# Recurrence stage: GpSimd builds an item's tree right after its decays, the limits follow the next item's statistics, and two norms of norms come from one variance

## The reference

```python
x = x + _L0_attn_ref(_layernorm(x), ...)   # its own layer norm again, projections, softplus, a state scan of 64 states a channel
x = x + _L0_ffn_ref(_layernorm(x), ...)    # x @ expert_w[0].T + expert_b[0]
x = x + _L1_attn_ref(_layernorm(x), ...)   # layer norm again, k, v, sigmoid decays and reads; per head (8 of 64 x 64):
                                           #   state = (1 - w_t)[:, None] * state + k_t v_t ;  out = r_t . state
x = x + _L1_ffn_ref(_layernorm(x), ...)    # layer norm again, signs -> best of 8 clusters, best of its 8 tiles (argmax),
                                           #   the row's 8 values of that tile, min and max of each tile over all rows, a spline
```

## Time and profile before

| what | value |
|---|---|
| median of 3 runs | 8956.1 us (8954.75 to 8961.61) |
| the profiled execution's own time | 8956.13 us |
| its span in the profile | 8954.3 us |
| busy over the span | PE 7718.1 us (86%), DVE 7107.0 (79%), POOL 5805.7 (65%), ACT 4707.2 (53%) |
| pre stage, 0 to 560 us | DVE 305.55 us busy, PE 338.37, POOL 32.64 |
| scan stage, 600 to 5560 us | DVE 4801.94 us busy, POOL 4779.56, PE 4554.60 |
| mid stage, 5571 to 7073 us | PE 1432.18 us busy, DVE 438.29, granted clock 0.99 |
| recurrence stage, 7092 to 8732 us | DVE 1395.19 us busy, PE 1290.36, POOL 779.33, granted clock 0.79 |

### The profile page before, as it was taken

The page is one execution under the profiler, slowest core; times in us unless marked ns, Lnnn a source line. Parts: engine busy times, 40 slices in busy tenths (PEclk is TensorE's granted clock), DMA queues, the critical chain, the costliest instruction groups (busy, mean ns, idle before and its releaser), DMA issues. The chain is left out here.

```text
span 8954.3 us, 223728 instructions
## 1 busy us (share of the span) xinstructions
PE 7718.1 (86%) x76550; PEld 5688.4 (64%) x76550; DVE 7107.0 (79%) x8782; ACT 4707.2 (53%) x10584; POOL 5805.7 (65%) x3304
## 2 busy tenths in 40 slices
PE   5659989999989899999999998899999877778774
PEld 3337777777777777777777776444444455555552
DVE  5549999999999999999999998323323488888876
ACT  4447777777777777777777776111111122222220
POOL 0019999999999999999999998000000144444444
PEclk8779999999999999999999999999999887777875
DMA  3340000000000000000000001122212211121115
GB/s 129 136 149 0 20 20 19 0 20 20 0 20 20 20 0 20 20 10 9 20 20 0 20 5 58 61 84 75 89 67 88 83 61 60 63 63 63 61 47 172
DMA packets 198781, 423.45 MB, mean 47 GB/s; under 512 B 22448, under 2 KB 48496, under 8 KB 183024
## 3 DMA queue, kind: packets, MB, share of 16 engines
q1 hardware_dynamic: 172768, 382.77, 12.7%
q10 hardware_dynamic: 25872, 38.80, 1.2%
HBM read 225.11 MB, written 196.41 MB: 47 GB/s over the span
## 5 line engine op out<-in xcount | busy, mean ns | idle before, releaser
L453 POOL TENSOR_TENSOR scan_hc<-scan_h,scan_cb 128x1024 f32<-128x1024 f32 x2048 | 4779.6, 2369 | 253.1 <-DMA scan_cb<-scratch_bc 117.6
L619 DVE TENSOR_TENSOR_SCAN scan_h<-scan_a,scan_carry,scan_u 128x512 f32<-128x512 f32 x4096 | 4801.9, 1261 | 156.1 <-PE scan_u L558 125.3
L558 PE MATMUL scan_u<-scan_dg,scan_v 64*128 64x128 f32 x32768 | 2391.7, 286 | 340.0 <-DVE scan_h L619 280.1
L504 ACT ACTIVATE scan_a<-scan_dt,scan_aneg 128x512 f32<-128x512 f32 x4096 | 2659.5, 708 | 44.4 <-issue 30.1
L558 PEld LDWEIGHTS scan_u<-scan_dg,scan_v 64*128 64x128 f32 x32768 | 2000.7, 188 | 820.0 <-DVE scan_h L619 538.1
L566 PE MATMUL scan_y<-scan_ident,scan_hc 128*128 128x128 f32 x16408 | 2250.4, 280 | 59.5 <-POOL scan_hc L453 33.6
L566 PEld LDWEIGHTS scan_y<-scan_ident,scan_hc 128*128 128x128 f32 x16408 | 1764.3, 141 | 309.7 <-POOL scan_hc L453 34.5
L475 ACT ACTIVATE scan_dg<-scan_half,scan_bt 128x64 f32<-128x64 f32 x4096 | 1138.7, 341 | 5.3 <-DVE scan_onward L602 5.2
L144 POOL TENSOR_TENSOR mid_r<-mid_ve,mid_half_neg 128x4 f32<-128x4 f32 x48 | 48.5, 1011 | 1269.0 <-DVE mid_ve L129 1269.0
L496 ACT ACTIVATE scan_carry<-scan_h,scan_onward 128x4 f32 (+1 forms) x1008 | 302.9, 301 | 1043.1 <-DVE scan_h L619 1043.1
L1223 DVE TENSOR_TENSOR core_rk<-core_rr,core_k 128x128 f32<-128x128 f32 (+7 forms) x512 | 409.0, 799 | 0.0
(11 more groups left out here) (211 smaller groups left out, 8209.8 us busy)
## 6 DMA issues: line engine op xcount, KB each, us to landing
scratch_y<-scan_yo ACTq DMA_DIRECT2D x17, 1024.0 KB, 4.7
pre_x<-in_x SPq DMA_DIRECT2D x16, 1024.0 KB, 6.9
scratch_z<-pre_zt SPq DMA_DIRECT2D x16, 1024.0 KB, 3.9
scratch_dt<-pre_dt SPq DMA_DIRECT2D x16, 1024.0 KB, 4.6
scratch_vr<-pre_vr ACTq DMA_DIRECT2D x16, 1024.0 KB, 4.7
scan_dt<-scratch_dt SPq DMA_DIRECT2D x16, 1024.0 KB, 5.3
scan_v<-scratch_vr SPq DMA_DIRECT2D x32, 512.0 KB, 7.7
scan_z<-scratch_z SPq DMA_DIRECT2D x16, 1024.0 KB, 10.7
```

The source lines that it names most:

```text
L453: pool.tensor_tensor(hc[:, q].rearrange("p n (r j) -> p n r j", j=P), h[:, q].rearrange("p n (r j) -> p n r j", j=P), cb[:, bass.ds(b * NS ...
L504: ins = act.activation(a[:, q, n, :], dt[:, par, q, :], ACT.Exp, scale=aneg[:, q, bass.ds(m * 2 + n, 1)])
L558: mm = pe.matmul(u_ps[:, q % 2, g, k * HP:(k + 1) * HP, :], v[row, par, k, q, :], dg[row, buf, k], start=True, stop=True)
L619: ins = dve.tensor_tensor_scan(h[:, q, n, :], a[:, q, n, :], u_ps[:, q % 2, :, :, n].rearrange("p g t -> p (g t)"), carry[:, q, bass.ds(m ...
```

## The change

In `pre_phase` and `mid_phase` the second norm takes no statistics of its own. The mean of a normalized row is 0 and its variance v / (v + eps), so both scalings in one are (x - mean) / sqrt(v (1 + eps) + eps^2). `pre_phase` makes both `ve` rows from one variance (`both_stats`), one root of twice the width, and then `zh` and `z` from x (`both_norms`); the piece with the statistics stands where the first norm stood, and the one with root and rows where the second stood. `mid_phase` calls `norm_dve` once, with `twice`, in place of its third and fourth norm.

In `core_phase` GpSimd makes the tree of item i + 3 in turn i, which is the item whose decays VectorE makes in that same turn. The work is cut in two pieces around `pick`, and `total` is a third piece, one turn later, behind `root`. On VectorE the sum of `pr` and the limits leave `route` and come behind the next item's statistics, before its root is waited for. `pr` is stored element by element instead of tile by tile. All leads of the stage grow by one (the limits have lead 0, the rest 1 to 5); between the other pieces nothing moves. In leads of before, the order in turn i is now: GpSimd `root(i)`, `totals(i+2)`, `keys(i+3)` (five products), `pick(i)`, `more_keys(i+3)` (ten products); VectorE `state(i)`, `norms(i)` (statistics only), `limits(i-1)`, `centred(i)` (L1200 to L1207), `decays(i+3)`, `spread_scores(i+2)`, `route(i)`.

```diff
+NORM_BOTH = 10
+BOTH_VE = 4
+
+
+def both_stats(dve, ticks, cnt, x, st, mv, ve, tiles):
+
+    for j in range(tiles):
+        last = dve.bn_stats(st[:, j, :], x[:, j, :])
+    cnt.link(dve, last)
+    hold(dve, ticks)
+    for j in range(tiles):
+        last = dve.bn_aggr(mv[:, j, :], st[:, j, :])
+    cnt.link(dve, last)
+    cnt.inc(dve.tensor_scalar(ve[:, 0], mv[:, :, 1], EPS, None, ALU.add))
+    cnt.inc(dve.tensor_scalar(ve[:, 1], mv[:, :, 1], 1.0 + EPS, EPS * EPS, ALU.mult, ALU.add))
+
+
+def both_norms(dve, cnt, roots, item, root_n, outs, x, mv, ve, r0, rr, tmp, tiles):
+
+    roots.wait(dve, item, root_n)
+    cnt.link(dve, dve.tensor_tensor(tmp, r0, r0, ALU.mult))
+    cnt.link(dve, dve.tensor_tensor(tmp, tmp, ve, ALU.mult))
+    cnt.link(dve, dve.tensor_scalar(tmp, tmp, -0.5, 1.5, ALU.mult, ALU.add))
+    cnt.link(dve, dve.tensor_tensor(rr, r0, tmp, ALU.mult))
+    for e in (1, 0):
+        for j in range(tiles):
+            last = dve.tensor_scalar(outs[e][:, j, :], x[:, j, :], mv[:, j, 0:1], rr[:, e, j:j + 1], ALU.subtract, ALU.mult)
+        cnt.inc(last)
...
-            def first_norm(c, par, half):
+            def stats(c, par, half):
                 norm_steps.begin(c)
                 dve.wait_ge(x_in[par], (half + 1) * 16)
+                both_stats(dve, ticks_dve, norm_steps, x[:, par], st, mv, ve, J)
+
+            def norms(c, par, half):
 
                 pe_steps.wait_freed(dve, c)
-                norm_dve(dve, ticks_dve, norm_steps, root_steps, c, 1, z[:, par], x[:, par], st, mv, ve[:], r0[:], rr[:], tmp[:], J)
-
-            def second_norm(c, par, half):
-                norm_dve(dve, ticks_dve, norm_steps, root_steps, c, 2, zh[:, par], z[:, par], st, mv, ve[:], r0[:], rr[:], tmp[:], J)
+                both_norms(dve, norm_steps, root_steps, c, 1, (z[:, par], zh[:, par]), x[:, par], mv, ve[:], r0[:], rr[:], tmp[:], J)
...
-            skewed(dve, NCH, [(0, turned), (1, first_norm), (0, copies), (1, second_norm), (0, softplus)])
+            skewed(dve, NCH, [(0, turned), (1, stats), (0, copies), (1, norms), (0, softplus)])
...
-                norm(c, 3, h, x2[:, par])
-                norm(c, 4, x[:, par], h)
+                norm(c, 3, x[:, par], x2[:, par], twice=True)
...
-            pipelined(sp, ITEMS, [(4, load_decays), (2, load_rows), (0, store)])
-            after.wait_all(sp, ITEMS - 1)
+            pipelined(sp, ITEMS, [(5, load_decays), (3, load_rows), (1, store)])
+            routed.wait_all(sp, ITEMS - 1)
...
             def keys(i, par, m):
                 pool_a.begin(i)
 
-                pe_b.wait_freed(pool, i)
-
-                after.wait(pool, i - 2, S_STATE)
+                pe_b.wait(pool, i - 2, B_OUT)
                 chain.wait_all(pool, i)
-
...
-                join(0)
-                half(1, 1)
-                half(1, 0)
+                pool_a.inc(join(0, par))
+                pool_a.inc(half(1, 1, par))
+                pool_a.inc(half(1, 0, par))
                 pool_a.wait(pool, i, 1)
-                join(1)
-                last = widen(1)
+                pool_a.inc(join(1, par))
+                pool_a.inc(widen(1, par))
+
+            def more_keys(i, par, m):
+                last = 5
                 for l in range(2, LEVELS):
                     pool_a.wait(pool, i, last)
-                    join(l)
-                    last = widen(l)
-                    half(l, 1)
-                    half(l, 0)
+                    if l + 1 < LEVELS:
+                        pool_a.inc(join(l, par))
+                    last = pool_a.inc(widen(l, par))
+                    pool_a.inc(half(l, 1, par))
+                    pool_a.inc(half(l, 0, par))
                 pool_a.wait(pool, i, last)
                 for kind, src, dst in ((1, rk[:, par, SUB], steps(kl[:, par])), (0, first[:, par, 0:SUB], ql[:, par])):
                     f = far[LEVELS][:, kind * C:(kind + 1) * C].rearrange("p (o c) -> p o c", o=1).broadcast_to([P, SUB, C])
                     pool_a.inc(pool.tensor_tensor(dst, src, f, ALU.mult))
 
+            def totals(i, par, m):
+                totaled.begin(i)
+
+                after.wait(pool, i - 2, S_STATE)
+                totaled.inc(join(LEVELS - 1, par))
+
             def pick(i, par, m):
 
                 after.wait(pool, i, S_OH)
                 hold(pool, ticks_pool)
-                pool_b.inc(pool.tensor_tensor(pr[:].rearrange("p (n e) -> p n e", e=8), xf[:].rearrange("p (n e) -> p n e", e=8),
+                pool_b.inc(pool.tensor_tensor(pr[:].rearrange("p (e n) -> p n e", e=8), xf[:].rearrange("p (n e) -> p n e", e=8),
                                               oh[:, bass.ds(par * (L // P) + m, 1), :].rearrange("p o (n e) -> p (o n) e", e=1).broadcast_to([P, NT, 8]), ALU.mult))
-            pipelined(pool, ITEMS, [(0, root), (2, keys), (0, pick)])
+            pipelined(pool, ITEMS, [(1, root), (3, totals), (4, keys), (1, pick), (4, more_keys)])
...
-                pool_a.wait_all(dve, i)
+                totaled.wait_all(dve, i)
...
+            def centred(i, par, m):
                 pool_b.wait(dve, i, 1)
...
+            def limits(i, par, m):
+                routed.begin(i)
+                at = lambda t: t[:, bass.ds(par * (L // P) + m, 1), :].rearrange("p o n -> p (o n)")
+
                 pool_b.wait_all(dve, i)
                 hold(dve, ticks_dve)
-                after.link(dve, dve.tensor_reduce(at(xs), pr[:].rearrange("p (n e) -> p e n", e=8), AX.X, ALU.add))
+                routed.link(dve, dve.tensor_reduce(at(xs), pr[:].rearrange("p (e n) -> p e n", e=8), AX.X, ALU.add))
                 hold(dve, ticks_dve)
-                after.inc(dve.tensor_reduce(mm2[:, 0:1], at(xs), AX.X, ALU.max))
-                after.link(dve, dve.tensor_reduce(mm2[:, 1:2], at(xs), AX.X, ALU.min, negate=True))
+                routed.inc(dve.tensor_reduce(mm2[:, 0:1], at(xs), AX.X, ALU.max))
+                routed.link(dve, dve.tensor_reduce(mm2[:, 1:2], at(xs), AX.X, ALU.min, negate=True))
 
                 for e in range(2):
-                    after.inc(dve.scalar_tensor_tensor(out=ext[:, e, :], in0=pen[:], scalar=mm2[:, e:e + 1], in1=ext[:, e, :], op0=ALU.min, op1=ALU.max))
-                after.wait(dve, i, after.n)
-            pipelined(dve, ITEMS, [(0, state), (0, norms), (3, decays), (2, spread_scores), (0, route)])
+                    routed.inc(dve.scalar_tensor_tensor(out=ext[:, e, :], in0=pen[:], scalar=mm2[:, e:e + 1], in1=ext[:, e, :], op0=ALU.min, op1=ALU.max))
+                routed.wait(dve, i, routed.n)
+            pipelined(dve, ITEMS, [(1, state), (1, norms), (0, limits), (1, centred), (4, decays), (3, spread_scores), (1, route)])
...
```

More of the change, by code:

```diff
@@ L117, in hold, with norm_dve @@
     eng.sem_inc(ticks, 1)
-def norm_dve(dve, ticks, cnt, roots, item, root_n, out, x, st, mv, ve, r0, rr, tmp, tiles):
+def norm_dve(dve, ticks, cnt, roots, item, root_n, out, x, st, mv, ve, r0, rr, tmp, tiles, twice=False):
     for j in range(tiles):
@@ L128, in norm_dve @@
     cnt.link(dve, last)
-    cnt.inc(dve.tensor_scalar(ve, mv[:, :, 1], EPS, None, ALU.add))
+    if twice:
+        cnt.inc(dve.tensor_scalar(ve, mv[:, :, 1], 1.0 + EPS, EPS * EPS, ALU.mult, ALU.add))
+    else:
+        cnt.inc(dve.tensor_scalar(ve, mv[:, :, 1], EPS, None, ALU.add))
     roots.wait(dve, item, root_n)
@@ L1097, in root, with join @@
                 pool_b.inc(pool.tensor_tensor(r0[:], ve[:], half_neg[:], ALU.pow))
+            def join(l, par):
+                e = ends(l, par)
+                n = C >> l
+                left, right = e[:, 1:n:2], e[:, n:2 * n:2]
+                if l + 1 == LEVELS:
+                    return pool.tensor_tensor(total[:, par], left, right, ALU.mult)
+                left, right = (t.rearrange("p (c e) -> p c e", e=2) for t in (left, right))
+                return pool.tensor_tensor(pair_ends(joint[l + 1][:]), left, right, ALU.mult)
@@ L1437, in outputs @@
                 pe_b.inc(mm)
-            pipelined(pe, ITEMS, [(1, tree), (1, turn_keys), (2, products), (0, turn_x), (1, reads), (2, turn_scores), (0, tile_scores), (1, sums), (1, outputs)])
+            pipelined(pe, ITEMS, [(2, tree), (2, turn_keys), (3, products), (1, turn_x), (2, reads), (3, turn_scores), (1, tile_scores), (2, sums), (2, outputs)])
 def final_phase(nc, D, N, x3_s, oh_s, xs_s, ext_s, table_d, grid_d, ident_d, out_d):
```

62 lines of the change are left out of this document (28 added, 34 removed).

## The result

The changed kernel takes 8649.8 us (median of 4 runs, 8644.1 to 8653.7), beside it the kernel before 8958.9 (8954.8 to 8963.2): ratio 0.9654, 95% interval 0.9638 to 0.9671. The profiled execution has a span of 8647.0 us.

What follows compares the result with a forecast made beforehand. VectorE's list, stretched beside GpSimd's tree, was taken to set the 25.35 us recurrence turn. From 8956.1 us, 233 (59 turns at 21.4) and 12 (pre and mid) were subtracted: 8711 us, own range 8680 to 8760, wider range 8655 to 8830.

Steps and rivals of the forecast that it cites:

- 12 forecast: Pre and mid: the first item saves 5.1 us and 7.1 us of norm work, together 12 us; steady turns gain nothing.
- Of the rivals the first: Recurrence stage: TensorE becomes the bound at the low clock, its stretch stays at 17.1 us; 8850 us, chance 8%.
- the second (all of VectorE excludes GpSimd): Recurrence stage: every VectorE instruction excludes GpSimd's products, turn 26.8 us, slower at 9032 us; chance 3%.
- the third: Recurrence stage: exclusion moves only in part, tree some 2 us longer in its new place; 8823 us, chance 12%.
- the fifth: Recurrence stage: the tree's new place gives nothing, VectorE's wait equals the old stretching; 8944 us, chance 2%.
- At 13.0, y ends at 6.0: Recurrence turn: TensorE's stretch from `turn_x`, begun at -7.0, takes 13.0 us, so y ends 6.0 us after `own`.
- 11.4 for VectorE to resume: Recurrence turn: after `ve`, limits and GpSimd's root, VectorE starts the Newton pieces 11.4 us behind `own`.
- 21.4: Recurrence stage: mean turn after the change, 21.15 us plus 0.25 for slow TensorE stretches, against 25.35 before.
- the remainder of the turn before: Recurrence turn: adding up the old turn gave 25.1 against 25.35 measured; that 0.25 us was added to the new turn.
- the 60th turn that was not counted: Recurrence stage: of 60 intervals from item 3 to item 63 the first was taken as lost, so 59 counted.
- the forecast's tie: TensorE: slow stretches follow about 6 us of idle ahead of `turn_x`; mean idle falls from 5.2 to 2 us.
- The fourth rival: Recurrence stage: limits hide entirely, no slow stretch, GpSimd alone sets a turn of 20.35 us; 8649 us, chance 10%.

Runs made afterwards that it cites:

- e1: Kernel before with only the norms of norms made from one variance, recurrence stage code unchanged: 8946.0 us, ratio 0.9985 to the kernel before.
- b1: Changed kernel with `ve` made by two instructions with one SBUF tensor each instead of one with two: 8627.9 us.
- e4: Changed kernel with GpSimd's tree back at its old place behind `root`, limits still moved: 8807.8 us.
- e9b: Changed kernel with two added matmuls of 512 columns at the head of `turn_x`, lengthening TensorE's stretch to y: 8688.4 us.
- e8: Kernel before with four added matmuls of 512 columns ahead of TensorE's wait for `xf`, filling its idle time: 8963.4 us in one run.
- b2: Changed kernel with the last two products of GpSimd's tree (`kl` and `ql`) put behind the next turn's root: 8657.8 us.

## Why the prediction was wrong in size

The main mechanism was right: GpSimd's tree no longer lies on VectorE's decays. Row by row: the decays take 7.2 us from first product to `own`, the first of them 0.28, Newton to decays 2.2, tree with `pick` ends 9.7 behind `own`; the wait at the sum of `pr` is gone; root is waited for 1.84 us; `ve` is held (1.41). x3, the statistics and the spread are not stretched. Pre and mid gave 14.2 by e1, 12 forecast. Of the rivals the first is out (stretches over 15 us are 10 of 63, not all), the second (all of VectorE excludes GpSimd) by b1, the third by the tree's end at 9.7, the fifth by e4.

The step that failed is "At 13.0, y ends at 6.0" and what hung on it: TensorE's stretch was taken too long, so the limits were put on the path in every turn, 11.4 for VectorE to resume. Measured, the stretch takes 12.25 us or less in 42 of 63 turns, 20 of these 10.5, which no turn of before had in its steady part. With y at 3.5 to 5.2, in 38 of 60 turns, the limits end 8.5 to 10.0 behind `own`, the root ends last at 10.35, and the turn is 19.8. e9b makes y late again and gets turns of 20.2 to 22.0, mean 21.17. By parts, of the 0.86 us between 21.4 and 20.54: the turn with y at 6.3 is 20.7 where the forecast added up 20.9 and 0.25 for 6.0, so the addition was 0.45 too long or more (0.25 of it is the remainder of the turn before, carried over without a row); the ordinary turns (19.8 and 20.7) have a mean of 20.0, another 0.7 less; and those over 22 us cost 0.55 instead of 0.25. The 0.7 needed the shorter stretch, but not that alone. By the forecast's own terms a turn set by the root would last 10.2 + 0.8 + 2.2 + 7.2 + 0.25 = 20.65; it lasts 19.8, since the root ends at 10.35 and not at 11.0 and nothing of the 0.25 shows. That VectorE resumes at 11.3 in the turn of 20.7, close to the 11.4, is partly luck: `ve` ends at 9.7, not 8.9, held until GpSimd's last product ends, and the limits then need 1.5 us and don't wait for the root. 60 x 0.86 and the 60th turn that was not counted (3.95) are the 56 us missed in the stage.

Why the stretch is shorter shows in the granted clock. Three stretches of the changed kernel, 10.5, 13.3 and 16.7 us long (windows, columns as above):

```profile
7622.60:7633.10 10.50, 10.50 (x85) 7.59 (x87) 9.87 (x27) 2.14 (x4) 3.51 (x7) 1.00 0.26 76
7642.30:7655.60 13.30, 13.27 (x82) 9.24 (x84) 10.09 (x27) 2.14 (x4) 6.22 (x12) 0.74 0.25 79
7682.80:7699.50 16.70, 16.67 (x83) 12.22 (x85) 10.28 (x27) 2.13 (x4) 8.26 (x14) 0.59 0.18 63
```

The same instructions at clocks of 1.00, 0.74 and 0.59, that is all, half and little at 2.4 GHz. The forecast took the durations of before, at a mean clock of 0.79 and with 5.2 us of idle ahead of each stretch, and weighed that idle only for the stretches over 15 us. With less idle the ordinary ones were shorter too, as e8 shows in the kernel before. Stretches over 15 us did not vanish (10 of 63 here, 15 of 63 before, where the forecast counted 16 of 62, and 16 in e8).

The idle ahead of each of the three stretches tells them apart:

```profile
7622.55 0.65 PE L1440 MATMUL core_kt_ps<-core_ident,core_xf 128*128 128x128 f32 x4 [1.41 <-DVE core_xf L1252]
...
7642.33 0.65 PE L1440 MATMUL core_kt_ps<-core_ident,core_xf 128*128 128x128 f32 x4 [3.10 <-DVE core_xf L1252]
...
7682.83 0.65 PE L1440 MATMUL core_kt_ps<-core_ident,core_xf 128*128 128x128 f32 x4 [3.10 <-DVE core_xf L1252]
```

In the changed kernel this has no exception: all 18 stretches behind an idle of 3.1 us took 13.2 to 16.7, the 45 others (idle at most 1.6) 10.5 to 13.7. And each idle of 3.1 us follows a stretch of 10.5: a fast stretch makes TensorE wait for `xf`, and the next one is slow. So the mean idle of 1.8 us hid what the forecast's tie needed, the idle of the single turn. That tie is not the whole cause either. In e8 all 16 stretches over 15 us came behind idles of 2.2 to 2.7, but eleven others behind such idles took 12.0 to 13.3; in b2 TensorE idled 1.9 to 2.0 us in each steady turn and no stretch there passed 12.9. What decides between 13.2 and 16.7 stays open. The Trainium skill (TensorE: Matmul & The Clock Gate, HAM oscillation) names the idle between bursts; e8's rise from 0.79 to 0.87 and the 18 stretches agree, but no page or run here tells the 13.2 from the 16.7.

The fourth rival gave 8649 us, by way of a turn of 20.35 without long stretches. Its time is met by luck: its way, GpSimd alone sets the turn, holds in 38 of 60 turns, which last 19.8, and turns of 20.7 and 23.1 make up the rest; `ve` is held after all.
